# Four graph layers on one core: running sums of layers 1, 2 and 4 as scans over rows that ScalarE has turned

## The chip, the cores and the metric

One Trainium2 chip, one of its cores. The metric is the time of one execution of the program on the device, in microseconds (us); lower is better.

## The reference, cut to what matters

6250 nodes with 64 numbers each go through four layers; 106250 edges, sorted by destination, are shared by all. Each layer sums messages over the edges into a node, and the result is added to x and normalised.

```
x = _layernorm(x + _L0_gnn_ref(x, L0_gnn_weight, src, dst, edge_type_16), axis=-1)
x = _layernorm(x + _L1_gnn_ref(x, L1_gnn_beta, src, dst), axis=-1)
x = _layernorm(x + _L2_gnn_ref(x, edge_index, L2_gnn_W_l, L2_gnn_W_r, L2_gnn_att, L2_gnn_bias), axis=-1)
x = _layernorm(x + _L3_gnn_ref(x, L3_gnn_W, L3_gnn_coeff, L3_gnn_h_bias, L3_gnn_loop_weight, src, dst, edge_type_8), axis=-1)
...
    out = jax.ops.segment_sum(m, dst, num_segments=feat.shape[0])                         # L0: m = x[src] @ w[edge type]
    out = jax.ops.segment_sum(alpha[:, None] * x[col_index], row_index, num_segments=N)   # L1: softmax of cosines
    agg = jax.ops.segment_sum(msg, dst, num_segments=n_nodes)                             # L3: 2 bases x 64 numbers an edge
```

## The kernel before

The edges are padded to 128 x 832: each partition holds 832 edges in a row (columns), and the columns are worked on in 52 chunks of 16 (`CH`, `NCH`). A segment sum is a running sum along the columns that starts anew where `gf` is 0: row j becomes row j-1 times `gf[j]` plus the message of column j. The running sums are stored to DRAM (`s0` to `s3`), and the row at each node's last edge is fetched from there.

All order is fixed by hand: each engine has its own program, and semaphores (`S[...]`) join them. The names in this text count layers from 1; the code counts from 0 (`L0` to `L3`).

- **Layer 1**, `linear_chunk_g/_v/_y`. POOL issues 16 indirect DMAs a chunk (`gather`, L190), one a column, from the table `y0` into a ring of 8 chunk buffers (`ring0`, `N0`). DVE makes the running sum in place, 16 dependent instructions a chunk (L514), each of which waits for the one before by the semaphore `lin0`. SP stores the chunk. POOL may fill a buffer again once the chunk 8 before is stored and the first row of the chunk 7 before is summed. The first 5 chunks (`FR`) go another way, over TensorE. Beside chunks 5 to 30 DVE and TensorE count edges a node: `hist_v` (L364, L366), then 16 matmuls of `hist_t` (L372), two such steps a chunk, and DVE's next step waits for TensorE's last (semaphore `hpe0`). `twin_v` (L2062) are tests of symmetry, two a chunk to chunk 31.
- **Layer 2**, `layer1_v`. POOL gathers into 4 chunk buffers (`G1`). `fill1` (L779) spreads the destination's row over its edges (16 dependent instructions a chunk, in PSUM), `soft1` (9 steps, L800 to L820) makes the logits and the running maximum, ACT takes the exponential (`exp1_a`, L828), `px1` (L838, L839) multiplies, and `step1` (L850) is the running sum of 65 numbers, 16 dependent instructions. They are interleaved on DVE.
- **Layer 3** (`layer2_*`) is not touched.
- **Layer 4**, `basis_chunk_v`. POOL gathers into 4 chunk buffers (`GB`), which `L1663`, the product with the two coefficients of an edge type, sets free. Ahead of it stand L1650, L1652 and L1655 (the coefficients), behind it 16 dependent instructions of 128 numbers (L1673). Beside chunks 8 to 14 `loop3_v` takes in products of x that TensorE made (`turn3_t`, `turn3_a`, `loop3_t`).

The two steps of the code that matter most:

```
v.scalar_tensor_tensor(out=buf[:, j, :], in0=buf[:, j - 1, :] if j else prev[:, CH - 1, :],
                       scalar=gf[:, c * CH + j:c * CH + j + 1], in1=buf[:, j, :],
                       op0=ALU.mult, op1=ALU.add).then_inc(S["lin0"], 1)
```

## Time and profile before

| what | value |
|---|---|
| times without a profile, 3 runs | 6202.34 us median (6194.47 to 6212.94) |
| time of the profiled execution | 6149.63 us |
| its span, first to last instruction | 6147.8 us |
| DVE busy | 2871.9 us, 47% |
| POOL busy | 3520.1 us, 57% |
| PE busy | 1595.5 us, 26% |
| ACT busy | 1115.1 us, 18% |

The profiled execution is 52.7 us shorter than the median of the runs without a profile. No engine is busy throughout: a share of busy time is a mean over four layers with different limits, so each layer is to be read by itself, by what its engines wait for.

### The profile page before, as it was taken

How to read it: one execution, taken by the hardware profiler on the slowest of the kernel's cores; microseconds unless marked ns; L12 is line 12 of the kernel's file. 1: busy time of each engine (PE TensorE's matmuls, PEld its weight loads, DVE VectorE, ACT ScalarE, POOL GpSimd, SP SyncE). 2: the span in 40 equal slices, each digit the busy share in tenths (PEclk: the TensorE clock that was granted, in tenths of full speed). 3: DMA queues.
4: the chain of work that ended last, by engine and by line, in shares of the span. 5: the costliest groups of instructions: out<-in, count | busy, mean ns of one | idle time of the engine just before them, and what ended most of it. 6: DMA issues, size and time to landing. Idle time of an engine off the chain costs nothing.

```text
span 6147.8 us, 31588 instructions
## 1 busy us (share of the span) xinstructions
PE 1595.5 (26%) x6543; PEld 813.1 (13%) x6543; DVE 2871.9 (47%) x7562; ACT 1115.1 (18%) x3419; POOL 3520.1 (57%) x3636
## 2 busy tenths in 40 slices
PE   5531110000000000002375566666664500000002
PEld 1421110000000000001122222222221400000001
DVE  2344444125354455544255565555556632444344
ACT  1100000000000000001155555555555400000000
POOL 5355666766666666664634544454442576676754
PEclk7765555555555555556687888888887655555555
DMA  4212222221222222221123333333334221222222
GB/s 140 105 53 62 65 67 72 72 67 61 51 72 65 64 70 72 69 67 37 49 103 122 140 139 129 125 140 139 129 124 157 67 67 54 65 79 76 67 68 72
DMA packets 185944, 529.62 MB, mean 86 GB/s; under 512 B 70454, under 2 KB 75170, under 8 KB 169480
## 3 DMA queue, kind: packets, MB, share of 16 engines
q1 hardware_dynamic: 65816, 395.51, 17.0%
q0 software_dynamic: 117696, 129.81, 10.5%
q10 hardware_dynamic: 2224, 2.13, 0.1%
q14 instruction: 151, 1.24, 0.1%
q8 instruction: 57, 0.93, 0.1%
HBM read 185.57 MB, written 341.44 MB: 86 GB/s over the span
## 4 chain that ended last, share of the span: by engine, by line
DVE 39%; another core or an unknown queue 24%; issue 18%; PE 11%; ACT 5%; POOL 3%; DMA 1%; DVEq 0%; ACTq 0%; POOLq 0%; SPq 0%
DVE AR L1673 10%; DVE AR L514 5%; DVE ps L779 5%; PE ps L1220 4%; POOL AR L190 2%; PE ps L1236 2%; DVE AR L850 2%; DVE AR L1385 2%; ACT AR L1371 2%; DVE AR L364 1%; DVE AR L1663 1%; ACT AR L1227 1%; DVE AR L800 1%; PE ps L680 1%
## 5 line engine op out<-in xcount | busy, mean ns | idle before, releaser
L190 POOL DMA_INDIRECT AR<-xt,Si x2496 | 2402.0, 962 | 1687.3 <-issue 743.9
L190 POOL DMA_INDIRECT AR<-y,R x752 | 721.4, 959 | 520.9 <-issue 222.2
L1385 DVE SCALAR_TENSOR_TENSOR AR<-AR,gf 128x390 f32<-128x390 f32 x780 | 484.2, 621 | 654.3 <-ACT AR L1371 458.3
L1220 PE MATMUL ps<-AR,WLR 128*128 128x512 f32 x1248 | 681.7, 673 | 131.6 <-ACT AR L1227 88.2
L1673 DVE SCALAR_TENSOR_TENSOR AR<-AR,gf 128x128 f32<-128x128 f32 x831 | 295.0, 355 | 472.6 <-DVE AR L1673 360.1
L1371 ACT ACTIVATE AR<-AR 128x64 f32<-128x64 f32 x1664 | 495.5, 346 | 0.0
L1227 ACT ACTIVATE AR<-ps 128x512 f32<-128x512 f32 x624 | 368.5, 591 | 210.9 <-remote 146.7
L779 DVE SCALAR_TENSOR_TENSOR ps<-ps,gf,AR 128x64 f32<-128x64 f32 x831 | 242.2, 291 | 303.5 <-remote 160.5
L514 DVE SCALAR_TENSOR_TENSOR AR<-AR,gf 128x64 f32<-128x64 f32 x831 | 237.5, 286 | 258.2 <-DVE AR L514 155.5
L190 POOL DMA_INDIRECT AR<-s,endi x196 | 215.5, 1100 | 186.8 <-issue 112.4
L1220 PEld LDWEIGHTS ps<-AR,WLR 128*128 128x128 f32 x1248 | 238.8, 216 | 436.7 <-issue 312.5
L1354 DVE TENSOR_TENSOR AR<-AR,ps 128x512 f32<-128x512 f32 x416 | 282.8, 680 | 5.3 <-ACT ps L1329 5.3
L850 DVE SCALAR_TENSOR_TENSOR AR<-AR,gf 128x65 f32<-128x65 f32 x780 | 217.4, 279 | 100.7 <-remote 64.2
L1191 DVE SCALAR_TENSOR_TENSOR AR<-AR,gf 128x64 f32<-128x64 f32 x831 | 229.8, 277 | 48.4 <-DVE AR L1191 23.5
L364 DVE TENSOR_TENSOR AR<-AR,ps 128x1568 bf16<-128x1568 int32 x52 | 92.7, 1783 | 315.9 <-remote 291.4
L828 ACT ACTIVATE ps<-AR 128x17 f32<-128x17 f32 (+1 forms) x52 | 9.8, 188 | 1250.9 <-remote 431.8
L372 PE MATMUL ps<-AR 128*98 128x64 bf16 x832 | 80.1, 270 | 560.8 <-DVE AR L366 433.8
L1743 PE MATMUL ps<-ident,AR 128*128 128x128 f32 x1 | 0.5, 477 | 809.4 <-DVE AR L1673 809.4
L1992 ACT ACTIVATE AR<-AR 128x7 f32<-128x7 f32 x7 | 1.5, 208 | 1114.0 <-DVE AR L633 1067.9
L1236 PE MATMUL ps<-AR,A 128*32 128x512 f32 x1248 | 203.5, 604 | 0.0
L1016 PE MATMUL ps<-AR,ones 128*128 128x384 f32 (+1 forms) x6 | 3.7, 758 | 708.3 <-DVE AR L967 708.3
L1251 PE MATMUL ps<-ident,AR 128*128 128x128 f32 x208 | 55.3, 417 | 492.2 <-issue 319.1
(324 smaller groups left out, 2987.6 us busy)
## 6 DMA issues: line engine op xcount, KB each, us to landing
s<-AR SPq DMA_DIRECT2D x51, 3168.0 KB
AR<-xd SPq DMA_DIRECT2D x104, 512.0 KB
s<-AR SPq DMA_DIRECT2D x51, 1024.0 KB
AR<-xt,Si POOLq DMA_INDIRECT x2496
s<-AR SPq DMA_DIRECT2D x53, 512.0 KB
s<-AR SPq DMA_DIRECT2D x51, 528.0 KB
...
```

Of the source, the lines that this page charges most:

```text
L190: g.indirect_dma_start(out=o, out_offset=None, in_=table, in_offset=bass.IndirectOffsetOnAxis(ap=idx, axis=0)).then_inc(S[sem], 16)
L514: v.scalar_tensor_tensor(out=buf[:, j, :], in0=buf[:, j - 1, :] if j else prev[:, CH - 1, :], scalar=gf[:, c * CH + j:c * CH + j + 1], in1 ...
L779: v.scalar_tensor_tensor(out=xf1(c, j), in0=xf1(c, j - 1) if j else xf1(c - 1, CH - 1), scalar=gf[:, c * CH + j:c * CH + j + 1], in1=XBv[: ...
L850: v.scalar_tensor_tensor(out=Sv[:, j, 0:65], in0=Sv[:, j - 1, 0:65] if j else Sp[:, CH - 1, 0:65], scalar=gf[:, c * CH + j:c * CH + j + 1] ...
L1191: v.scalar_tensor_tensor(out=cur[:, j, D:P], in0=cur[:, j - 1, D:P] if j else prv[:, CH - 1, D:P], scalar=gf[:, c * CH + j:c * CH + j + 1] ...
L1220: t.matmul(PS[2 + k % 3][:], WLR[:, ch * P:(ch + 1) * P], XT2[:, u % 6, :], start=True, stop=True).then_inc(S["pm"], 1)
L1227: s.activation(RL2[:, u % 5, ch * 512:(ch + 1) * 512], PS[2 + k % 3][:], ACT.Relu).then_inc(S["ar"], 1)
L1236: m = t.matmul(PS[6][32 * q:32 * q + 32, :], w_, m_, start=(ch == 0), stop=(ch == 3))
L1354: v.tensor_tensor(s2v(c)[:, cols, 0:n * 65].rearrange("p j (h d) -> p j h d", h=n)[:, :, :, 0:D], bc(xsv(c)[:, cols, 0:D].unsqueeze(2), [P ...
L1371: s.activation(Sv[:, j, h * 65:h * 65 + D], xsv(c)[:, j, 0:D], ACT.Copy, scale=pe_[:, h, j:j + 1]).then_inc(S["ap"], 1)
L1385: m = v.scalar_tensor_tensor(out=Sv[:, j, 0:HW], in0=Sv[:, j - 1, 0:HW], scalar=gf[:, c * CH + j:c * CH + j + 1], in1=Sv[:, j, 0:HW], op0= ...
L1673: v.scalar_tensor_tensor(out=cur[:, j, :], in0=cur[:, j - 1, :] if j else prv[:, CH - 1, :], scalar=gf[:, c * CH + j:c * CH + j + 1], in1= ...
```

## The change

In layers 1 (from chunk 5 on), 2 and 4 a chunk's 16 dependent row instructions become few scans. A scan (`tensor_tensor_scan`) runs along 512 elements in memory, state times gate plus element. For that the 16 columns of one of the 64 features must lie side by side, so:

- `gates_a` (ACT) spreads a chunk's `gf` over a PSUM bank, 480 elements; element 0 of each group of 16 stays 0, set once by `memset`.
- `turned0_a`, `turned1_a` (ACT) copy a chunk of 1024 from (column, feature) to (feature, column). In layer 4, and for the sum of layer 2, no such copy is there: DVE's own product writes turned (L950, L1837 of the changed kernel; they answer to L838 and L1663).
- DVE adds the carry of the chunk before into column 0 (`carry0_v`, the first steps of `fill1` and `step1`, in `basis_v`), and then scans: 2 of 512 a chunk in layer 1; 2 for `fill1` and 2 and one of 16 for `step1` in layer 2; 4 in layer 4.
- `summed0_a`, `summed1_a`, `summed3_a` (ACT) copy the sums back to (column, feature), and SP stores when that copy is done (semaphore `co`) rather than when DVE's last row is.
- POOL fills a buffer of layer 1 again when the chunk 8 before is stored; it waits for nothing of the chunk 7 before. In layers 1 and 4 the last chunk is two units of 8 columns; in layer 2 its second half isn't taken apart from the first any more.
- ACT's program, which in layer 1 had nothing in this stretch and in layer 2 the exponentials alone, gets these copies; in layer 4 `turn3_a` moves in among them. DVE gets `memset`s of 11 PSUM banks. In layer 1 DVE's `hist_v` now stands behind the scans.

```diff
+        def gates_a(bank, at, n):
+            return s.copy(bank[:].rearrange("p (d j) -> p d j", j=n)[:, :, 1:n],
+                          bc(gf[:, at + 1:at + n].unsqueeze(1), [P, 512 // n, n - 1]))
+        def gates0_a(e, i):
...
+            if n == CH and i >= 2:
+                e.wait_ge(S["sc"], scans_upto(UN0, D, i - 1))
+            gates_a(gx0(i), c * CH + j0, n).then_inc(S["gx"], 1)
+        def turned0_a(e, i):
...
+            if i >= 2:
+                e.wait_ge(S["st"], i)
+            s.copy(t0v(i), ring0(c)[:, j0:j0 + n, :].rearrange("p j d -> p d j")).then_inc(S["cx"], 1)
+        def summed0_a(e, i):
+            c, j0, n = UN0[i]
+            e.wait_ge(S["sc"], scans_upto(UN0, D, i + 1))
+            s.copy(ring0(c)[:, j0:j0 + n, :], t0v(i).rearrange("p d j -> p j d")).then_inc(S["co"], 1)
+        def carry0_v(e, i):
+            c, j0, n = UN0[i]
+            e.wait_ge(S["cx"], i + 1)
+            if i:
+                e.wait_ge(S["sc"], scans_upto(UN0, D, i))
+                row = t0v(i - 1)[:, :, UN0[i - 1][2] - 1]
...
+            v.scalar_tensor_tensor(out=t0v(i)[:, :, 0], in0=row, scalar=gf[:, c * CH + j0:c * CH + j0 + 1],
+                                   in1=t0v(i)[:, :, 0], op0=ALU.mult, op1=ALU.add).then_inc(S["st"], 1)
+        def scan0_v(e, i):
...
+            for k in range(n * D // 512):
+                part = TT0[:, i % 2, k * 512:(k + 1) * 512]
+                v.tensor_tensor_scan(part, gx0(i)[:], part, 0.0, ALU.mult, ALU.add).then_inc(S["sc"], 1)
...
         def linear_chunk_g(e, tab, idx, c):
...
             if c >= N0:
                 e.wait_ge(S[f"s_{b}"], 16 * (c // N0))
-                e.wait_ge(S["lin0"], lin_at(c - N0 + 1, 0))
+                if c - N0 + 1 < FR:
+                    e.wait_ge(S["lin0"], lin_at(c - N0 + 1, 0))
+                elif c - N0 + 1 == FR:
+                    e.wait_ge(S["st"], 1)
...
+        def summed1_a(e, c):
+            e.wait_ge(S["sc"], raised("sc", 1) + 3 * (c + 1))
...
+                s.copy(Sv[:, j:j + n, 0:65], sum1(c)[:, :, j:j + n].rearrange("p d j -> p j d")).then_inc(S["co"], 1)
...
+            v.tensor_tensor_scan(PS[2 * (c % 2) + i - 1][:], gx1(c)[:], TX1[:, c % 2, (i - 1) * 512:i * 512], 0.0,
+                                 ALU.mult, ALU.add).then_inc(S["f1"], 1)
...
-            v.tensor_tensor(Sv[:, :, 0:D], Gv[:, :, 0:D], bc(pe_.unsqueeze(2), [P, CH, D]), ALU.mult).then_inc(S["p1"], 1)
...
+            v.tensor_tensor(sum1(c)[:, 0:D, :].rearrange("p d j -> p j d"), Gv[:, :, 0:D],
+                            bc(pe_.unsqueeze(2), [P, CH, D]), ALU.mult).then_inc(S["p1"], 1)
...
+            lo, n = (i - 1) * 512, 512 if i < 3 else CH
+            part = SUM1[:, c % 2, lo:lo + n]
+            v.tensor_tensor_scan(part, gx1(c)[:, 0:n], part, 0.0, ALU.mult, ALU.add).then_inc(S["sc"], 1)
...
             if c >= NBUF:
-                e.wait_ge(S["m3"], 4 * (c - NBUF + 1))
+                e.wait_ge(S["m3"], c - NBUF + 1)
...
+        def basis_v(e, i):
...
+            v.tensor_tensor(sum3(i).rearrange("p (b d) j -> p j b d", b=NBS), bc(rows.unsqueeze(2), [P, n, NBS, D]),
+                            bc(CW3[:, i % 2, :, 0:n].rearrange("p b j -> p j b").unsqueeze(3), [P, n, NBS, D]),
+                            ALU.mult).then_inc(S["m3"], 1)
...
+            for k in range(n * W3 // 512):
+                part = SUM3[:, i % 2, k * 512:(k + 1) * 512]
+                v.tensor_tensor_scan(part, gx3(i)[:], part, 0.0, ALU.mult, ALU.add).then_inc(S["sc"], 1)
+                if more and k == 0:
+                    weight3_v(e, i + 1, 2)
...
             for c in range(NCH):
-                exp1_a(e, c)
+                if c + 2 < NCH:
+                    gates1_a(e, c + 2)
+                    turned1_a(e, c + 2)
+                if c + 1 < NCH:
+                    exp1_a(e, c + 1)
+                summed1_a(e, c)
...
-            for q in range(NG):
-                turn3_a(e, q)
+            gates3_a(e, 0)
+            for i, (c, j0, n) in enumerate(UN3):
+                if 6 <= c < 6 + NG:
+                    turn3_a(e, c - 6)
+                if i + 1 < len(UN3):
+                    gates3_a(e, i + 1)
+                summed3_a(e, i)
...
+            for bank in (2, 3, 4, 5):
+                v.memset(PS[bank][:], 0.0).then_inc(S["init"], 1)
```

DVE's program in layer 1 beside the counting of edges, before; `k_hpe0` is TensorE's signal, `k_g_5` the landing of a gather:

```order
L364 TENSOR_TENSOR AR<-AR,ps 128x1568 [waits k_hpe0]
L366 TENSOR_TENSOR AR<-AR,ps 128x1024
L364 TENSOR_TENSOR AR<-AR,ps 128x1568 [waits k_hpe0]
L366 TENSOR_TENSOR AR<-AR,ps 128x1024
L2062 SCALAR_TENSOR_TENSOR AR<-AR 128x832 [waits k_v] x2
L514 SCALAR_TENSOR_TENSOR AR<-AR,gf 128x64 [waits k_lin0,k_g_5]
L514 SCALAR_TENSOR_TENSOR AR<-AR,gf 128x64 [waits k_lin0] x15
```

The same place in the changed kernel, from one carry to the next (the scans are printed as SCALAR_TENSOR_TENSOR of 512; L2257 and L2254 are tests of the kind of L2062):

```order
L546 SCALAR_TENSOR_TENSOR AR<-AR,gf 128x64 [waits k_sc,k_cx]
L2257 TENSOR_SCALAR AR<-Dd 128x832
L2254 TENSOR_SCALAR AR<-AR 128x832 [waits k_v]
L555 SCALAR_TENSOR_TENSOR AR<-ps,AR 128x512 [waits k_gx,k_st]
L555 SCALAR_TENSOR_TENSOR AR<-ps,AR 128x512
L365 TENSOR_TENSOR AR<-AR,ps 128x1568 [waits k_hpe0]
L367 TENSOR_TENSOR AR<-AR,ps 128x1024
L365 TENSOR_TENSOR AR<-AR,ps 128x1568 [waits k_hpe0]
L367 TENSOR_TENSOR AR<-AR,ps 128x1024
```

The 16 rows of L514 are gone; in their place stand a carry, which waits for ACT's turned copy (`k_cx`), and two scans; the counting moved behind them.

ACT's program in layer 1 in the changed kernel, three chunks of 47; before, no row stands there:

```order
L515 COPY ps<-gf 128x32x15 [waits k_sc,k_init]
L530 COPY AR<-AR 128x1024 [waits k_st,k_g_1]
L535 COPY AR<-AR 128x1024 [waits k_sc]
L515 COPY ps<-gf 128x64x7 [waits k_init]
L530 COPY AR<-AR 128x1024 [waits k_st,k_g_2]
L535 COPY AR<-AR 128x1024 [waits k_sc]
```

Each L535 waits for DVE's scans of its chunk (`k_sc`), and the next chunk's L530 is behind it.

DVE's program in layer 4, one chunk before:

```order
L1650 TENSOR_TENSOR ps<-AR,ps 128x128 [waits k_m3]
L1652 TENSOR_TENSOR AR<-ps,co 128x256 [waits k_m3]
L1655 TENSOR_REDUCE ps<-AR 128x32 [waits k_m3]
L1663 TENSOR_TENSOR AR<-AR,ps 128x2048 [waits k_m3,k_s_1,k_g_3]
L1673 SCALAR_TENSOR_TENSOR AR<-AR,gf 128x128 [waits k_lin3,k_m3]
L1673 SCALAR_TENSOR_TENSOR AR<-AR,gf 128x128 [waits k_lin3] x15
```

and one chunk of the changed kernel:

```order
L1837 TENSOR_TENSOR AR<-AR,ps 128x16x128 [waits k_co,k_cf,k_g_2]
L1806 TENSOR_TENSOR ps<-AR,ps 128x128
L1845 SCALAR_TENSOR_TENSOR AR<-AR,gf 128x128 [waits k_sc,k_m3]
L1809 TENSOR_TENSOR AR<-ps,co 128x256 [waits k_cf]
L1855 SCALAR_TENSOR_TENSOR AR<-ps,AR 128x512 [waits k_gx,k_st]
L1812 TENSOR_REDUCE ps<-AR 128x32 [waits k_cf]
L1855 SCALAR_TENSOR_TENSOR AR<-ps,AR 128x512 x3
```

The product (L1837) no longer has the coefficients' three steps ahead of it: those of the next chunk (L1806, L1809, L1812) stand between its carry and its scans.

## Rows read from the trace of the kernel before

**Rows 1.** By stretch: us; busy PE, PEld, DVE, ACT, POOL (instructions); clock, DMA, GB/s.
```profile
416.00:1041.00 625.00, 77.76 (x809) 71.00 (x808) 296.67 (x581) 0.00 (x0) 378.15 (x400) 0.50 0.22 63
1041.00:1403.00 362.00, 1.20 (x4) 1.00 (x4) 104.85 (x372) 0.00 (x0) 236.43 (x240) 0.50 0.27 84
1543.00:2802.00 1259.00, 1.46 (x4) 1.00 (x4) 626.70 (x2244) 16.88 (x104) 787.70 (x833) 0.50 0.26 66
2802.00:4867.00 2065.00, 1223.03 (x4694) 546.88 (x4694) 1129.32 (x2752) 1018.71 (x3133) 990.93 (x983) 0.79 0.34 117
4867.00:6062.00 1195.00, 30.32 (x123) 26.03 (x123) 477.07 (x1059) 3.85 (x13) 796.96 (x832) 0.50 0.23 68
```

**Rows 2.** Timeline of POOL around the counting of edges: start, us, what [idle before].
```profile
1028.70 0.94 POOL L190 DMA_INDIRECT AR<-y,R  x1 [0.30 <-issue]
1029.95 0.94 POOL L190 DMA_INDIRECT AR<-y,R  x1 [0.30 <-issue]
1041.59 0.94 POOL L190 DMA_INDIRECT AR<-y,R  x1 [10.69 <-DVE AR L514]
```

**Rows 3.** What POOL waited for in layers 1, 2 and 4: us, times, longest.
```profile
POOL AR L190 <- DVE AR L514: 140.8, 18, 15.1
...
POOL AR L190 <- DVE AR L839: 181.1, 16, 18.3
...
POOL AR L190 <- DVE AR L1663: 115.4, 15, 21.2
```

**Rows 4.** Timeline of POOL: first fetch of nodes' rows behind layers 1, 2, 4.
```profile
1406.58 1.03 POOL L190 DMA_INDIRECT AR<-s,endi  x1 [55.73 <-issue]
...
2804.25 0.94 POOL L190 DMA_INDIRECT AR<-s,fixg  x1 [40.25 <-DMA s<-AR]
...
6064.70 0.94 POOL L190 DMA_INDIRECT AR<-s,endi  x1 [34.55 <-DMA s<-AR]
```

**Rows 5.** By short stretch: us; busy DVE (instructions); clock, DMA, GB/s.
```profile
1111.00:1313.00 202.00, 41.19 (x145) 0.50 0.24 67
1383.00:1403.00 20.00, 17.54 (x62) 0.50 0.56 223
1708.00:1749.00 41.00, 11.23 (x39) 0.50 0.18 36
1749.00:1762.00 13.00, 12.72 (x47) 0.50 0.37 112
4972.00:5084.00 112.00, 36.22 (x80) 0.50 0.23 64
5386.00:5414.00 28.00, 25.88 (x58) 0.50 0.30 98
```

**Rows 6.** Timeline of DVE, counting of edges and sums.
```profile
1011.42 1.21 DVE L366 TENSOR_TENSOR AR<-AR,ps 128x1024 bf16<-128x1024 int32 x1
1035.71 1.79 DVE L364 TENSOR_TENSOR AR<-AR,ps 128x1568 bf16<-128x1568 int32 x1 [23.08 <-remote]
...
1040.56 5.13 DVE L514 SCALAR_TENSOR_TENSOR AR<-AR,gf 128x64 f32<-128x64 f32 x16
```

**Rows 7.** Groups of DVE by line: count, busy us, mean ns, idle before.
```profile
L1314 DVE TENSOR_TENSOR_SCAN AR<-AR 128x96 f32<-128x96 f32 x52 | 18.2, 350 | 0.0
...
L810 DVE TENSOR_TENSOR_SCAN AR<-Bn,AR 128x16 f32<-128x16 f32 x52 | 9.8, 189 | 18.1 <-remote 13.8 <-issue 2.2 <-DVE AR L807 2.0
...
L838 DVE TENSOR_TENSOR AR<-AR,ps 128x1024 f32<-128x1024 f32 x52 | 63.0, 1211 | 0.3 <-ACT AR L829 0.2 <-issue 0.2
```

**Rows 8.** Groups of ACT by line: contiguous and strided copies.
```profile
L1212 ACT COPY AR<-ps 128x512 f32<-128x512 f32 x208 | 122.0, 587 | 78.6 <-remote 28.3 <-PE ps L1205 27.9 <-issue 20.3
...
L1335 ACT COPY AR<-AR 128x96 f32<-128x96 f32 x52 | 18.1, 348 | 0.0
L1330 ACT ACTIVATE AR<-AR 128x102 f32<-128x102 f32 x51 | 14.0, 274 | 0.0
```

**Rows 9.** Timeline of the PE's counting step.
```profile
1012.69 1.54 PE L372 MATMUL ps<-AR 128*98 128x64 bf16 x16 [8.37 <-DVE AR L366]
```

More of the change, by code:

```diff
@@ L614, in stored_all @@
         def stored_all(e, L, n):
-            more = (16, 48, 48, 16)[L]
+            more = (16, 16, 48, 16)[L]
             for b in range(n):
@@ L1624, in build @@
         E8 = arena(6200, NC).bitcast(I32)
+        UN3 = [(c, 0, CH) for c in range(NCH - 1)] + [(NCH - 1, 0, CH // 2), (NCH - 1, CH // 2, CH // 2)]
+        W3 = NBS * D
+        SUM3 = arena(9100, 2, CH * W3)
         OH3 = PS[0][:, 64:64 + CH * R3].rearrange("p (j r) -> p j r", r=R3)
@@ L1677, in basis_chunk_y @@
-        def basis_chunk_y(e, c):
-            n = CH // 2 if c == NCH - 1 else CH
-            for j in range(0, CH, n):
-                e.wait_ge(S["lin3"], lin_at(c, j + n - 1))
-                load(e, columns_view(s3, c * CH + j, n), s3v(c)[:, j:j + n, :].rearrange("p j d -> p (j d)"), f"s_{c % 3}")
+            at = c * CH + j0
+            rows = GB[:, b, :].rearrange("p (j d) -> p j d", j=CH)[:, j0:j0 + n, :]
+            more = i + 1 < len(UN3)
+            if j0:
+                e.wait_ge(S["late"], 16 * CH + 16 * n)
+            else:
+                e.wait_ge(S[f"g_{b}"], gathered_before(3, b) + 16 * CH * (c // NBUF) + 16 * n)
@@ new lines, in basis_v @@
+            if i:
+                e.wait_ge(S["sc"], raised("sc", 3) + scans_upto(UN3, W3, i))
+                v.scalar_tensor_tensor(out=sum3(i)[:, :, 0], in0=sum3(i - 1)[:, :, UN3[i - 1][2] - 1],
+                                       scalar=gf[:, at:at + 1], in1=sum3(i)[:, :, 0],
+                                       op0=ALU.mult, op1=ALU.add).then_inc(S["st"], 1)
+            if more:
+                weight3_v(e, i + 1, 1)
+            if i:
+                e.wait_ge(S["st"], raised("st", 3) + i)
@@ L1868, in _ @@
                 load(e, rows_view(xt3, sl), X[:, sl, :].rearrange("p l d -> p (l d)"), "xt")
-            for c in range(NCH):
-                basis_chunk_y(e, c)
+            for i in range(len(UN3)):
+                basis_chunk_y(e, i)
             for q, (l0, n) in enumerate(G3):
@@ L1989, in _ @@
                 raw_first_a(e, u)
+            gates0_a(e, 0)
+            for i in range(len(UN0)):
+                if i + 1 < len(UN0):
+                    gates0_a(e, i + 1)
+                turned0_a(e, i)
+                summed0_a(e, i)
             for q in range(NG):
@@ L2116, in _ @@
                 linear_chunk_v(e, c)
+            for bank in (2, 3, 4, 5):
+                v.memset(PS[bank][:], 0.0).then_inc(S["init"], 1)
             masks_v(e, vc, 0)
```

346 lines of the change are left out of this document (221 added, 125 removed), and 2 rows, old and new, of the table names.

## The prediction

> **What bounds the kernel now.** I read the busy time by stretch first. In layers 1, 2 and 4 no engine is near full: POOL is the busiest with 0.61, 0.63 and 0.67 of its stretches, DVE has 0.47, 0.50 and 0.40 [rows 1]. Layer 3 (2802 to 4867 us) is the only one where TensorE and ACT work hard, and the change does not touch it. So the question for the other three is whether POOL's busy share is its limit. The timeline of POOL says it is: gathers start every 1.25 us (0.94 busy, 0.30 of issue) with nothing waited for [rows 2]. A layer of 832 gathers therefore takes at least 832 x 1.25 = 1040 us, a chunk of 16 takes 20.0 us. The chunks take 21.0 us in layer 1 ((1403 - 416) / 47), 24.2 in layer 2 (1259 / 52) and 23.0 in layer 4 (1195 / 52) [rows 1]. The excess is POOL waiting for a buffer that DVE has not set free, 140.8, 181.1 and 115.4 us [rows 3], and a tail after the last gather: POOL's first fetch of nodes' rows comes 55.7, 40.3 and 34.6 us later [rows 4]. These six numbers, 568 us, are all that faster sums can win.
>
> Why does DVE fall behind at half its time busy? DVE alone, in short stretches, shows two paces [rows 5]. With POOL stopped or just started again: 62 instructions in 20 us, 47 in 13, 58 in 28, so 0.32, 0.28 and 0.48 us each, their own durations. With POOL at its full pace for some 20 us and more: 145 in 202 us, 39 in 41, 80 in 112, so 1.39, 1.05 and 1.40 us each, though the instructions last no longer. In that slow pace an instruction costs about 1.0 to 1.4 us whatever it does, unless it lasts longer itself. I don't know why, and need only that the price is by the instruction. TensorE feels it too: its 16 matmuls of a counting step are recorded in 1.54 us [rows 9], yet DVE's next step started 23.08 us later, 4.8 us after POOL's last gather (1030.9 to 1035.7), and POOL then stood for 10.69 us until DVE had a row summed [rows 2, 6]. That pattern comes back about every 50 us and two chunks to 1040 us, and sets layer 1's first part.
>
> **The change part by part.** The number of DVE instructions falls, and they get longer.
>
> A scan of 512 is not in the trace. Scans of 16 and 96 last 189 and 350 ns [rows 7], 2.0 ns an element; 350 + 416 x 2.0 = 1.18 us is the value I take. Bounds: 0.8 us (at 1.18 ns an element, L838's 1211 ns for 1024 [rows 7]) and 2.4 us (twice).
>
> ACT's copies: 512 contiguous elements out of PSUM last 587 ns [rows 8], so 0.55 us for the 480 gates and at least 1.1 us for 1024. A strided copy of 96 elements lasts 348 ns, a contiguous activation of 102 lasts 274 [rows 8]: if some 0.19 us of both is fixed, 1.65 against 0.82 ns an element. The turned copies read or write at strides of 16 and 64 numbers, so I take 1.9 us for 1024, 3.6 for 2048, bounds 1.1 and 1.9 below. The same doubt holds for DVE's products that now write turned (L838, 1211 ns for 1024 [rows 7], and L1663 with 2048, so about 2.3): no loss to twice, 1.2 and 2.3 us more a chunk; I take half. A rule bears on this: the Trainium skill, SBUF — State Buffer, in "Door 1: The DMA port swizzle", says that SBUF is read in lines of 16 bytes and that each access which moves to another line costs, with a stride of four fp32 as the limit. It speaks against the change: by it every turned copy and product pays in full. ACT's two rows agree with it as far as they go; no row here shows DVE at such a stride.
>
> *Layer 1, chunks 5 to 30, with the counting.* Removed a chunk: 16 row instructions, 5.1 us in the fast pace [rows 6]. Added: carry 0.3, two scans 2.4. But the counting steps stay, and DVE waits for TensorE in them as before, until POOL pauses. POOL may now go one chunk further before it pauses (it needs the store of the chunk 8 before, not a row of the chunk 7 before), and after the pause it waits for carry, scans, ACT's copy back and the store, some 12 us instead of 6. So a cycle is 4.8 + 12 + 20 for each chunk, 57 us for two or 77 for three, 25.6 to 28.5 a chunk against 25 now; the chunk gained in the ring is worth 20 us once. I set this part at nothing; bounds: 60 us lost (three more a chunk, less the 20) and 100 won (if DVE is through before the slow pace sets in).
>
> *Layer 1, chunks 31 to 51.* Now 16 x 1.39 = 22.2 us a chunk, a little over POOL's 20.0. After: 3 instructions of DVE (4.2 us) and 3 of ACT (about 2 each), one behind the other, 10 to 12 us. POOL goes on at its pace, which it mostly has here already, and the backlog that makes the tail is gone: carry, scan, copy back, store for half a chunk, about 8 us instead of 55.7. Won: 47 us.
>
> *Layer 2.* DVE's instructions a chunk fall from 43 to 19 (4 and 4 in place of 16 and 16; 11 stay). Slow pace: 19 x 1.05 = 20 to 19 x 1.4 = 27 us, against 43 x 1.05 = 45 now. Fast: about 11.5 us of durations. So DVE is at or a little over POOL's 20.0 in the slow pace; it loses some 2 to 7 us a chunk, the ring of four takes that up for 10 chunks or more, then a short pause brings the fast pace, in which DVE makes up a chunk. I leave 45 of 181.1 us of waiting: won 136. ACT's five copies and exponentials (some 5 us, each dispatched apart) have a chunk's time; the turned copy of chunk c+2 is asked for after four of DVE's steps of chunk c, about when it is ready. Tail: nine short steps, exponential, product, scans, copy, store, about 15 us instead of 40.3: won 25. Together 161; bounds 80 and 195.
>
> *Layer 4.* Slow pace now: 20 instructions x 1.40 = 28 us a chunk. After: product 2.3 to 4.6, eight others x 1.4 = 11.2, so 14 to 16 us, under 20.0. POOL is the bound except for chunks 8 to 14. There TensorE's products (22 instructions for each), ACT's `turn3_a`, which now stands ahead of the gates for the next chunk, and `loop3_v` follow one another, about 25 to 30 us a chunk in the slow pace; the ring takes up 60 of it. I leave 35 of 115.4: won 80. Tail: half a product, carry, two scans, copy, store, about 10 instead of 34.6: won 25. Together 105; bounds 40 and 135.
>
> *Added.* 11 `memset`s of a PSUM bank, some 0.6 us each like a DVE operation of 512: 6 us if nothing hides them. Layer 3 and the node stages move but keep their length.
>
> Sum: 47 + 161 + 105 - 6 = 307 us. Against the profiled execution's own time, 6149.6 us, that is 5843 us. The median without a profile is 52.7 us above it, and I carry that over: 5895 us.
>
> **The rivals.**
>
> *The waits go further than I say.* If DVE slips through the counting cycles and the ring takes up layer 4's middle, up to 100 + 35 + 45 us more are won: 5720 to 5790. For it: the cycle has slack of few us. Against: TensorE's step is untouched and takes the wait over.
>
> *Strided work and ACT eat the gain.* Twice the time for scans, products and copies adds in layer 2 about 8 us a chunk to DVE; DVE is then at 28 to 35 us in the slow pace and waits come back: layer 2 wins 60, layer 4 50, layer 1 20: about 6070. This is what the rule above would make of it if DVE pays in full and more. Against: even so DVE has fewer steps than now.
>
> *Slower.* Now the chain of layer 1's sums never leaves DVE. After, each chunk goes ACT, DVE, ACT. If ACT's signal is held as TensorE's is in the counting, until POOL pauses and 4.8 us more [rows 2, 6], then every chunk costs 20.0 + 4.8 + some 2 us. The mean over the three layers is (987 + 1259 + 1195) / 151 = 22.8 us a chunk, which is where it decides; at 26.8 the kernel takes 151 x 4.0 = 600 us more, 6800 us. For it: TensorE's 23.08 us is real. Against: DVE's own signals came after 1.4 us in the same pace, TensorE has 32 instructions behind its one signal and ACT one; in layer 3 POOL gathers too and ACT does 3133 instructions in 2065 us [rows 1], though POOL is at 0.48 there.
>
> *It does nothing.* If the slow pace is by work and not by instruction, half the instructions at double length cost the same. Against: in layer 4's slow stretch an instruction is busy for 36.22 / 80 = 0.45 us and in its fast one for 25.88 / 58 = 0.45 us [rows 5]; the work is the same, only the time between steps is not.
>
> **How the numbers follow.** Main case 0.72, time 5790 to 6010. Further gain 0.08; strided work and ACT 0.12; slower 0.06; nothing 0.02. The range 5760 to 6060 takes in the first two and half of the third, and leaves 0.16 out. 0.3% (19 us) is about what a measurement of this kernel can tell from no change. Faster by more: 0.72 + 0.08 + 0.12, less a little for mishaps of its parts: 0.91. Within: 0.02. Slower: 0.07.
>
> **What would show it.** Right: POOL's starts 1.25 us apart through most of layers 2 and 4, the waits for L839 and L1663 down to some 45 and 35 us; first fetch of nodes' rows 8 to 15 us after the last gather; in the counting part still gaps of about 20 us ahead of `hist_v`; scans of 512 near 1.18 us. Wrong: if scans or turned products last over 2.4 us, if ACT's copies wait for each other so that DVE idles ahead of the carry, or if DVE after the change stands for ACT 20 us at a time. Above all my price by the instruction comes from stretches where DVE's steps depend on each other; if independent steps pay less, layer 2 wins more.

## The result, and the profile after

| | before | after |
|---|---|---|
| median, us | 6198.41 (6193.02 to 6212.94, 4 runs) | 6108.82 (6079.91 to 6118.44, 4 runs) |
| ratio | | 0.9841, 95% interval 0.9809 to 0.9874 |
| profiled execution / its span, us | 6149.63 / 6147.8 | 6079.91 / 6077.9 |

Faster, as forecast, but by 90 us where 303 were forecast: 6108.8 lies above the range (5760 to 6060). In the profiled pair the gain is 69.9 us of span; the profiled execution after lies 28.9 us below its median, so neither figure is exact to more than some 20 us.

By stretch, as [rows 1], shifted to where the same work now lies (us; busy PE, PEld, DVE, ACT, POOL; clock, DMA share, GB/s):

```profile
416.00:1070.00 654.00, 78.51 (x816) 71.79 (x816) 249.06 (x258) 105.98 (x75) 389.43 (x408) 0.50 0.21 61
1070.00:1366.00 296.00, 1.20 (x4) 1.00 (x4) 60.30 (x84) 86.86 (x63) 218.94 (x225) 0.50 0.31 97
1526.00:2717.00 1191.00, 2.25 (x6) 1.50 (x6) 562.35 (x1003) 241.84 (x262) 792.95 (x832) 0.50 0.27 70
2717.00:4817.00 2100.00, 1233.83 (x4692) 548.76 (x4692) 1127.00 (x2745) 1021.32 (x3131) 990.92 (x983) 0.78 0.33 115
4817.00:5980.00 1163.00, 31.33 (x125) 26.58 (x125) 493.28 (x501) 218.00 (x121) 836.36 (x833) 0.50 0.24 71
```

What POOL waited for in layer 1, and in layer 2, and in layer 4 from 4960 to 5960 us (us, times, longest), to set beside [rows 3]:

```profile
POOL AR L191 <- DMA s<-AR: 143.0, 8, 21.4
...
POOL AR L191 <- remote: 123.1, 20, 7.0
...
POOL AR L191 <- issue: 236.8, 711, 0.9
POOL AR L191 <- DVE AR L1837: 41.5, 3, 23.7
```

POOL's first fetches of nodes' rows, to set beside [rows 4]:

```profile
1371.02 1.55 POOL L191 DMA_INDIRECT AR<-s,endi  x1 [9.81 <-issue]
...
2719.10 0.94 POOL L191 DMA_INDIRECT AR<-s,fixg  x1 [27.98 <-DMA s<-AR]
...
5979.78 0.95 POOL L191 DMA_INDIRECT AR<-s,endi  x1 [11.26 <-DMA s<-AR]
```

The groups that the price list was about, to set beside [rows 7, 8]:

```profile
L1855 DVE TENSOR_TENSOR_SCAN AR<-ps,AR 128x512 f32<-128x512 f32 x208 | 242.5, 1208 | 156.6 <-issue 91.2 <-ACT ps L515 65.3
L950 DVE TENSOR_TENSOR AR<-AR,ps 128x1024 f32<-128x1024 f32 x52 | 98.7, 1898 | 0.1
L1837 DVE TENSOR_TENSOR AR<-AR,ps 128x2048 f32<-128x2048 f32 (+1 forms) x53 | 187.0, 3529 | 509.4 <-DMA AR<-xt,Si 509.4
...
L1796 ACT COPY AR<-AR 128x2048 f32<-128x2048 f32 (+1 forms) x53 | 189.3, 3572 | 725.6 <-issue 448.8 <-DVE AR L1855 276.8
L530 ACT COPY AR<-AR 128x1024 f32<-128x1024 f32 (+1 forms) x48 | 90.6, 1888 | 134.1 <-DMA AR<-y,R 134.1
L515 ACT COPY ps<-gf 128x480 f32<-128x480 f32 x153 | 85.4, 559 | 29.9 <-DVE ps L1024 17.9 <-DVE ps L2320 8.8 <-DVE ps L2421 3.2
```

The prices are close to those taken (scan 1.21 us, copies 1.89 and 3.57, gates 0.56, products 1.90 and 3.53 where I had about 1.8 and 3.4). So the loss lies elsewhere, and a ledger finds it. Each line of the table is the time between two fetches of POOL, before from [rows 2, 4] and the first gathers of layers 2 and 4 (1543.8 and 4867.4 us), after from the timeline above and the first gathers (1526.2 and 4817.8).

| stretch | before | after | gain | forecast |
|---|---|---|---|---|
| layer 1, to the nodes' fetch | 1406.6 | 1371.0 | 35.6 | 41 (47 less 6) |
| nodes behind layer 1 | 137.2 | 155.2 | -18.0 | 0 |
| layer 2 with its tail | 1260.5 | 1192.9 | 67.6 | 161 |
| nodes, layer 3, nodes | 2063.2 | 2098.7 | -35.5 | 0 |
| layer 4 with its tail | 1197.3 | 1162.0 | 35.3 | 105 |
| the rest, to the end of the span | 83.1 | 98.1 | -15.0 | 0 |

Layer 4 is the odd line. DVE hardly holds POOL up there: it waits for gathers 509.4 us (L1837, above), POOL waits for DVE 41.5 us, all before 5233 us. POOL's waits fell from 115.4 to 41.5 us, close to the 35 that I had left, and yet POOL needs 1162 us for work that I had put at 1040. The same queries in two halves of a stretch in which POOL waits for nothing, in the kernel after:

```profile
5233.00:5475.00 242.00, 0.00 (x0) 0.00 (x0) 135.68 (x136) 61.52 (x30) 183.66 (x192) 0.50 0.30 94
5475.00:5945.00 470.00, 0.00 (x0) 0.00 (x0) 194.03 (x189) 85.75 (x42) 349.57 (x336) 0.50 0.24 70
```

192 gathers in 242 us are 1.26 us each; 336 in 470 us are 1.40. The 1.40 is a mean: in a held chunk of 16, which takes 22.4 us, some gathers still start 1.25 us apart and others 1.40 to 2.1, so two rows of a timeline don't show it. The same split stands in the kernel before, behind the last pause of layer 1, and I had not looked:

```profile
1041.00:1262.00 221.00, 1.20 (x4) 1.00 (x4) 58.27 (x208) 0.00 (x0) 166.77 (x177) 0.50 0.27 79
1262.00:1350.00 88.00, 0.00 (x0) 0.00 (x0) 17.85 (x63) 0.00 (x0) 68.81 (x64) 0.50 0.24 71
```

177 gathers at 1.25, then 64 at 1.375 (the window begins a little before the slower pitch does; the last chunks take 22.4 us here too). This gives the theory that I tested.

**Theory A, a long-run limit.** A gather costs 1.40 us in the long run. At 1.25 us POOL runs ahead of that by 0.15 us a gather; after 11 or 12 chunks (some 190 gathers, 28 us ahead) it is held at 1.40, until a pause lets it run ahead again. While it is ahead, each DVE instruction costs 1.40 us (the theory as I tested it; the changed kernel's layer 4 goes against this part, see below). **Rivals:** B, 1.25 us is the floor and DVE's slow steps are what lengthens the layers, by the signal (B0), by the instruction (B1) or by their work (B2); C, DVE bounds layer 2 and only a longer pause makes it fast; D, the turned copies and products take the gain.

### The profile page after: what moved, and what is told of

The parts are those of the page before. It is cut to its first block and busy times, and to the rows that moved or that the text cites. A ratio compares the mean times of both kernels' runs of the same rounds, so it can differ in the third digit from the quotient of the medians.

```text
span 6077.9 us, 30032 instructions
## 1 busy us (share of the span) xinstructions
PE 1605.7 (26%) x6543; PEld 814.5 (13%) x6543; DVE 2732.0 (45%) x5146; ACT 1755.8 (29%) x3826; POOL 3568.6 (59%) x3636
## 3 DMA queue, kind: packets, MB, share of 16 engines
q0 software_dynamic: 117696, 129.81, 10.6%
## 5 line engine op out<-in xcount | busy, mean ns | idle before, releaser
L191 POOL DMA_INDIRECT AR<-xt,Si x2496 | 2447.7, 981 | 1605.6 <-issue 778.7
L1355 PE MATMUL ps<-AR,WLR 128*128 128x512 f32 x1248 | 696.1, 686 | 135.8 <-ACT AR L1362 95.7
L1837 DVE TENSOR_TENSOR AR<-AR,ps 128x2048 f32<-128x2048 f32 (+1 forms) x53 | 187.0, 3529 | 509.4 <-DMA AR<-xt,Si 509.4
L1796 ACT COPY AR<-AR 128x2048 f32<-128x2048 f32 (+1 forms) x53 | 189.3, 3572 | 725.6 <-issue 448.8
L1855 DVE TENSOR_TENSOR_SCAN AR<-ps,AR 128x512 f32<-128x512 f32 x208 | 242.5, 1208 | 156.6 <-issue 91.2
L535 ACT COPY AR<-AR 128x1024 f32<-128x1024 f32 (+1 forms) x48 | 90.0, 1875 | 644.6 <-DVE AR L555 494.8
L1326 DVE SCALAR_TENSOR_TENSOR AR<-AR,gf 128x64 f32<-128x64 f32 x831 | 230.1, 277 | 48.8 <-DVE AR L1326 24.6
```

The lines of the kernel that those rows point to most:

```text
L191: g.indirect_dma_start(out=o, out_offset=None, in_=table, in_offset=bass.IndirectOffsetOnAxis(ap=idx, axis=0)).then_inc(S[sem], 16)
L1326: v.scalar_tensor_tensor(out=cur[:, j, D:P], in0=cur[:, j - 1, D:P] if j else prv[:, CH - 1, D:P], scalar=gf[:, c * CH + j:c * CH + j + 1] ...
L1355: t.matmul(PS[2 + k % 3][:], WLR[:, ch * P:(ch + 1) * P], XT2[:, u % 6, :], start=True, stop=True).then_inc(S["pm"], 1)
L1796: s.copy(s3v(c)[:, j0:j0 + n, :], sum3(i).rearrange("p x j -> p j x")).then_inc(S["co"], 1)
L1837: v.tensor_tensor(sum3(i).rearrange("p (b d) j -> p j b d", b=NBS), bc(rows.unsqueeze(2), [P, n, NBS, D]), bc(CW3[:, i % 2, :, 0:n].rearra ...
L1855: v.tensor_tensor_scan(part, gx3(i)[:], part, 0.0, ALU.mult, ALU.add).then_inc(S["sc"], 1)
```

## The experiments

The first pair of traces and the six groups of runs below were each taken on a chip of their own, and the occasions are of two kinds: the kernel before took 6198, 6056, 6049 and 6144 us on four of these occasions and 4809 on three. I call the first kind of chip limited and the second quiet, but no chip was met twice, so these runs can't tell a property of the chip from a condition of the occasion; on one of the quiet chips a single one of 31 executions of the kernel before took 6614 us. Each run below is compared with the kernel before on its own chip.

The kept traces of the two kinds also differ in what they hold. A trace lists the updates of semaphores: there are 18726 to 23540 such records in each trace from a limited chip, and 75610 to 77676 in each from a quiet one, for the same numbers of DMAs and much the same instructions. In the held stretch above (5475 to 5945 us) there are 671, one every 0.70 us, for 336 gathers; in 500 us of the same kernel on a quiet chip there are 6999, for 398 gathers. So on limited chips updates either merge or go unrecorded, and it may be the recording itself that takes 0.70 us an event. That rival stands untested: none of these runs compares an execution that was recorded with one that wasn't.

Lengths of layers in the text run from POOL's first gather to the first fetch of nodes' rows behind it, by POOL's timeline of each run.

**1. Signals and instructions of DVE in layer 2** (limited chip, before 6056.14 us). `sig2` and `sig124` leave out signals whose waiters can take the next one:

```diff
-            v.tensor_tensor_scan(part, gx1(c)[:, 0:n], part, 0.0, ALU.mult, ALU.add).then_inc(S["sc"], 1)
+            m = v.tensor_tensor_scan(part, gx1(c)[:, 0:n], part, 0.0, ALU.mult, ALU.add)
+            if i == 3:
+                m.then_inc(S["sc"], 1)
...
-            m.then_inc(S["q1"], 1)
+            if i:
+                m.then_inc(S["q1"], 1)
```

> Same instructions as the changed kernel, but in layer 2 DVE signals 13 times a chunk instead of 18 (first half of the first product, the second product, the first scan of each group and the second of the last group signal no longer; who waited for them waits for the next signal of DVE). Theory A, the price is by the signal: in layer 2 the slow chunk of DVE took 26.63 us = 19 x 1.40; it falls by 5 x 1.40 to about 19.6 us, under POOL's 20.0 us a chunk, POOL's waits in layer 2 (123.1 and 28.0 us) fall under 40 and the kernel takes about 6000 us. Theory B, the price is by the instruction, or by the work: the slow chunk stays at 26.6 us and the time at 6109 +- 15 us.

> As sig2, and the scans of layers 1 and 4 signal once a chunk instead of two and four times. Theory A: as sig2 in layer 2; in layer 4 DVE already waits for POOL, so only a change of POOL's 22.4 us a chunk there could show, and if that pace comes from DVE's signals (9 a chunk, then 6) it falls toward 20.0 in the last 23 chunks, up to 50 us less than sig2. If it has another cause, sig124 equals sig2 within 20 us. Theory B: 6109 +- 15 us.

Measured: 5979.74 us (ratio 0.9871, 0.9836 to 0.9906) and 5986.76 (0.9878, 0.9843 to 0.9912). The slow chunk of DVE stays at 26.6 us in both (in parts of the layer every second one is 18.9), layer 2 takes 1198 and 1197 us, layer 4 1160 and 1160. The price is not by the signal, and layer 4's pace not DVE's doing. The unchanged kernel after was not run on this chip; the comparison is of chunks and layers with its first trace, and of the runs with each other.

`dumsig` and `dumno` add four one-element copies a chunk, with and without a signal:

```diff
+                for k in range(4):
+                    m = v.tensor_copy(dm[:, 4 * c + k:4 * c + k + 1], gf[:, 4 * c + k:4 * c + k + 1])
+                    m.then_inc(S["du"], 1)
```

> The changed kernel with four more DVE copies of one element a partition in each chunk of layer 2, each with a signal that nobody waits for. Theory A (by the signal): the slow chunk grows by 4 x 1.40 = 5.6 to 32.2 us, the kernel by some 200 to 280 us. Theory B1 (by the instruction): the same here, and the same in dumno. Theory B2 (by the work): the chunk grows by 4 x 0.06 us or so, the kernel by 0 to 15 us.

> The same four copies a chunk without signals. Theory A: the slow chunk stays near 26.6 us, the kernel grows by 0 to 15 us. Theory B1 (by the instruction): slow chunk 32.2 us, 200 to 280 us more. Theory B2: as A.

Measured: 5979.27 and 5968.84 us, one run each. In both the slow chunk grows from 26.6 to 32.2 us, by 4 x 1.40. Two slow stretches, `dumno` and then the kernel after:

```profile
1640.00:1672.20 32.20, 0.00 (x0) 0.00 (x0) 11.27 (x24) 4.62 (x5) 24.27 (x27) 0.50 0.25 59
```
```profile
1846.10:1872.70 26.60, 0.00 (x0) 0.00 (x0) 10.95 (x19) 4.63 (x5) 15.13 (x16) 0.50 0.23 56
1972.00:1982.10 10.10, 0.00 (x0) 0.00 (x0) 10.06 (x21) 4.61 (x6) 7.66 (x9) 0.50 0.43 129
```

19 instructions at 1.40 us are 26.6, 23 are 32.2 (the window also catches one of the next chunk); the last row is a chunk in the fast pace (with two of its neighbours' instructions). So in layer 2 B1's price is right, signal or none, but the 200 to 280 us that B1 put on the kernel did not come: both runs are within 11 us of `sig2`. The Trainium skill, VectorE: DVE Perf Modes, "The DRAIN you can't avoid", says that a semaphore behind each instruction adds nothing to a chain of DVE copies; these two runs agree, 32.2 us with and without. No theory of DVE's pace had the next number: layer 2 takes 1194 and 1193 us, as with chunks of 26.6. DVE's slow chunk got 5.6 us longer and the layer no longer. Something else fixes its length.

**2. A chip of the other kind** (before 4809.46 us). The unchanged kernel after, one one-byte memset behind each gather of layers 1, 2 and 4 in both kernels, and the copies and products contiguous (which then sums other elements):

```diff
                 gather(buf[:, j, :], xt3, Si[:, c * CH + j:c * CH + j + 1],
                        "late" if c == NCH - 1 and j >= CH // 2 else f"g_{b}")
+                g.memset(fl[:, 1 * flat[0]:1 * flat[0] + 1], 0)
+                flat[0] += 1
```
```diff
-            s.copy(tx1(c), XB1[:, c % 3, :].rearrange("p (j d) -> p d j", j=CH)).then_inc(S["cx"], 1)
+            s.copy(TX1[:, c % 2, :], XB1[:, c % 3, :]).then_inc(S["cx"], 1)
```

> The changed kernel once more, beside the others on their chip. Layers 1, 2 and 4 as in its first trace (1179, 1193 and 1162 us from first gather to the nodes' fetch); layer 3 was 2099 us there and 1997 to 2012 us in the four later runs whose layer 3 is the same code, so the time is expected at 5975 +- 25 us if layer 3 goes by the chip, 6100 if it goes by the kernel.

> The changed kernel with one POOL memset of one byte a partition behind each gather of layers 1, 2 and 4, so that gathers start some 1.35 to 1.5 us apart instead of 1.25. Theory A (backlog): in the long run a gather costs 1.40 us; at 1.25 POOL runs ahead by 28 us in 11 to 12 chunks, and while it is ahead every DVE instruction costs 1.40 us and TensorE's signals wait. Then with gathers 1.40 apart DVE never turns slow (chunk of 10 us in layer 2), the counting costs 22 to 24 us a chunk instead of 26.2, layers 2 and 4 keep their length within 30 us if the pitch is 1.40 to 1.43, and the time falls by 50 to 120 us; if the pitch is 1.5, each layer takes 832 x 1.5 = 1250 us and the time rises by up to 80. Theory B (1.25 is what a gather costs, DVE is slow while gathers run): DVE stays slow at 26.6 us a chunk and each layer gains 832 x 0.15 or more: 250 to 400 us slower.

> The same memset behind each gather in the kernel before. Theory A: DVE's 43 instructions a chunk in layer 2 take 12 us in the fast pace, its 16 row instructions of layer 4 10 us, so the kernel before becomes as fast as pace1 within 40 us. Theory B: DVE's slow chunks of 45 and 28 us stay, the kernel is at least 250 us slower than before.

> The changed kernel with ACT's copies and DVE's products of layers 1, 2 and 4 written and read contiguously instead of turned; the sums are then taken over other elements. Rival that strided work eats the gain: copies fall from 1.9 and 3.6 us to about 1.1 and 2.1, products from 1.9 and 3.5 to 1.2 and 2.3, and the time falls by 60 to 150 us. Theory A: POOL's 22.4 us a chunk stay, the time stays within 20 us.

Measured: after 4815.52 us (ratio 1.0010, 1.0001 to 1.0020), `pace1` 4817.14 (1.0014), `bpace1` 4811.08 (1.0002), `cont` 4814.95 (1.0011). My guess that layer 3 alone differs by chip was wrong: everything does. Two stretches of the kernel after on this chip, layer 2 and layer 4:

```profile
1205.00:2242.00 1037.00, 1.46 (x4) 1.00 (x4) 516.66 (x977) 235.06 (x257) 783.84 (x831) 0.50 0.31 79
3700.00:4745.00 1045.00, 31.32 (x125) 26.57 (x125) 493.27 (x498) 216.45 (x119) 783.09 (x823) 0.50 0.27 78
```

831 gathers in 1037 us: 1.25 us each to the end, the 1040 us of my floor. POOL waits for no buffer in layers 1, 2 and 4, DVE is never slow, the recorded signals of DVE in layer 2 come 0.01 us after the instruction's end (median), and the kernels before and after are equal to 0.1%. The memset fits into the 0.30 us between gathers, so `pace1` and `bpace1` told nothing of theory A. `cont` settles rival D for this kind of chip: turned against contiguous, copies take 1888 against 1025 ns and 3565 against 1865, products 1864 against 1214 and 3520 against 2247, and the time is the same. The Trainium skill, SBUF — State Buffer, "Door 1: The DMA port swizzle", is borne out in the durations (a factor of 1.5 to 1.9 beyond its stride) and costs nothing here: ACT and DVE have room under POOL's pace. `cont` was not run on a limited chip.

**3. Pacing POOL on a limited chip** (before 6049.37 us). Three memsets behind each gather, in both kernels; and a wait for two chunks' buffers at once:

```diff
+                for u in range(3):
+                    m = g.memset(fl[:, 3 * (c * CH + j) + u:3 * (c * CH + j) + u + 1], 0)
```
```diff
-                e.wait_ge(S["p1"], 2 * (c - 3))
+                e.wait_ge(S["p1"], 2 * (c - 3 + (c % 2 == 0)))
```

> The changed kernel again, as the measure for the other three on their chip. On a chip like that of the second call (4809 us for the kernel before, POOL's gathers 1.25 us apart throughout, signals 0.01 us late) it equals the kernel before within 0.3%. On a chip like that of the first two traces (signals at multiples of 0.70 us) it takes 1.2 to 1.6% less than the kernel before.

> The changed kernel with three one-byte POOL memsets behind each gather of layers 1, 2 and 4 (with one, they fitted into the 0.30 us between gathers and the pitch stayed at 1.25 us). Gathers then start about 1.40 to 1.6 us apart. On a chip of the slow kind: theory A (a gather costs 1.40 us there in the long run, POOL runs ahead at 1.25, and while it is ahead DVE pays 1.40 us an instruction and TensorE's signals wait): DVE is fast throughout layer 2 (10 to 12 us a chunk), the counting takes POOL's pace instead of 26.2 us a chunk, and with a pitch of p the three layers take about 832 x p each; at 1.45 the kernel is 20 to 80 us faster than without the memsets. Theory B (DVE is slow whenever gathers run): DVE's slow chunks of 26.6 us stay and the kernel is 250 us or more slower. On a chip of the quiet kind both expect 832 x (p - 1.25) more for each layer and nothing else.

> The same three memsets in the kernel before. Slow kind of chip, theory A: DVE fast throughout, so the kernel equals pace3 within 40 us and is faster than the kernel before by 60 to 150 us. Theory B: slower than the kernel before by 250 us or more. Quiet kind: as pace3.

> The changed kernel with POOL's wait in layer 2 taken for two chunks at once: ahead of every even chunk it waits until DVE has set free the buffers of two. Pauses become rarer and longer (12 us and more instead of 6.6). Slow kind of chip, theory A: the sum of the pauses is set by the 1.40 us a gather, so layer 2 keeps its 1193 us within 25, though DVE turns fast at other places. Theory C (a longer pause is what makes DVE fast, and DVE is what bounds the layer): layer 2 gets 40 to 100 us shorter. Quiet kind: nothing changes, within 20 us.

| | us | ratio to before | layer 1's counting ends | nodes 1 | layer 2 | layer 4 | rest |
|---|---|---|---|---|---|---|---|
| after_third | 5983.95 | 0.9895 (0.9860 to 0.9930) | 1073 | 154 | 1196 | 1159 | 97 |
| pace3 | 5917.94 | 0.9783 (0.9746 to 0.9821) | 938 | 138 | 1194 | 1183 | 83 |
| bpace3 | 5918.45 | 0.9789 (0.9757 to 0.9822) | 942 | 137 | 1193 | 1184 | 82 |
| pair | 5971.77 | 0.9873 (0.9840 to 0.9907) | 1084 | 154 | 1191 | 1160 | 98 |

The kernel after, unchanged, gains 1.05% here, a little less than the 1.2 to 1.6% that I had expected.

Adding 7,248 instructions to POOL makes both kernels faster, and makes them equal. Layers 2 and 4 in `pace3`, then in `bpace3` (a gather and three memsets are four POOL instructions):

```profile
1475.00:2607.00 1132.00, 0.00 (x0) 0.00 (x0) 498.27 (x942) 226.82 (x249) 901.06 (x3200) 0.50 0.27 69
4665.00:5815.00 1150.00, 30.16 (x122) 25.89 (x122) 484.57 (x487) 214.30 (x117) 922.56 (x3257) 0.50 0.24 70
```
```profile
1485.00:2620.00 1135.00, 1.46 (x4) 1.00 (x4) 583.76 (x2142) 16.23 (x100) 914.25 (x3197) 0.50 0.27 69
4664.00:5817.00 1153.00, 25.68 (x104) 22.09 (x104) 471.39 (x1049) 3.17 (x10) 924.34 (x3257) 0.50 0.24 70
```

3200 / 4 = 800 gathers in 1132 us, 1.415 each, with scans and (799 in 1135, 1.42) with row steps. POOL waits for no buffer in either; DVE, which has twice the instructions in `bpace3`, keeps up in both. The memsets themselves would make the pitch 1.27 us; here is `pace3` in layer 4, at that pitch and then held:

```profile
5600.28 0.94 POOL L192 DMA_INDIRECT AR<-xt,Si  x1
5601.23 0.17 POOL L1837 MEMSET fl<- 128x1 uint8 x3
5601.55 0.94 POOL L192 DMA_INDIRECT AR<-xt,Si  x1
5602.49 0.18 POOL L1837 MEMSET fl<- 128x1 uint8 x3
5603.32 0.95 POOL L192 DMA_INDIRECT AR<-xt,Si  x1 [0.65 <-issue]
5604.27 0.12 POOL L1837 MEMSET fl<- 128x1 uint8 x1
5605.21 0.10 POOL L1837 MEMSET fl<- 128x1 uint8 x1 [0.83 <-issue]
```

So with memsets POOL is held at 1.40 on the mean from the second chunk of a layer on, and never runs ahead; why they make it so I can't say. The rest follows theory A. DVE steps keep up, TensorE's signals come through (the counting's steps mostly follow one another every 11 to 13 us, where in the kernel after four come 5 to 7 us apart and then two of 27) and layer 1's first part ends 135 us earlier. Layer 2 keeps its length, layer 4 loses 24 us, about the 28 us ahead that it now starts without. `pair` agrees too: with pauses up to 13.5 us instead of 7.0, layer 2 takes 1191 us. That is against rival C, and so is `pace3`, where DVE is fast throughout and layer 2 is no shorter.

**4. What the 1.40 us belongs to, and the price of the remedy.** Layer 4's gathers fetch 64 rows from the fifth chunk on (the other 64 partitions keep old rows); the three memsets in layer 1 alone; `pace3` again:

```diff
-                gather(buf[:, j, :], xt3, Si[:, c * CH + j:c * CH + j + 1],
+                h = P if c < NBUF else P // 2
+                gather(buf[0:h, j, :], xt3, Si[0:h, c * CH + j:c * CH + j + 1],
```

> The changed kernel whose gathers of layer 4 fetch 64 rows instead of 128 from the fifth chunk on (the other 64 partitions keep older rows, so layer 4's result is another). On a chip of the slow kind: if the 1.40 us belongs to the rows of a gather (10.9 ns each), a half gather costs 0.70 us in the long run, POOL is never held and the chunks stay at 20 us or less throughout, so layer 4 takes some 50 us less than the 1160 us of the others. If it belongs to the gather, or to the POOL instruction, chunks turn to 22.4 us after 11 or 12 chunks as before and layer 4 keeps 1160 +- 15 us. On a quiet chip only the gather's own length shows.

> The changed kernel with the three memsets behind each gather of layer 1 alone. Theory A on a slow chip: layer 1 as in pace3 (1126 us instead of 1181), the nodes behind it as in pace3 (138 instead of 154), layers 2 and 4 as without memsets (1194 and 1160): 5905 to 5925 us, 0.990 of the changed kernel. If the gain of pace3 came from layers 2 or 4, it stays at 5984. On a quiet chip: 0 to 40 us slower than the kernel before.

> pace3 once more. Slow chip: 0.978 of the kernel before again. Quiet chip (1.25 us a gather without end): its pitch of 1.27 us costs 832 x 0.02 x 3 = 50 us at most, so 4810 to 4870 us.

Quiet chip, before 4809.28 us: 4777.20 (layer 4 1018 us, 19.3 a chunk to the end), 4826.51 (1.0035, 1.0022 to 1.0047) and 4856.34 (1.0096, 1.0079 to 1.0113). The remedy costs 1% where there is no limit. The first two once more:

> As half4, on another chip if one is met. On a chip of the slow kind: if the 1.40 us belongs to the rows of a gather (10.9 ns each), chunks of layer 4 stay at 20 us or less from the fifth on and layer 4 takes some 50 us less than 1160; if it belongs to the gather, chunks of 22.4 us come back and layer 4 keeps 1160 +- 15 us. On a quiet chip it repeats 4777 us.

> As pace_l1. Slow chip, theory A: 0.978 or less of the kernel before (layer 1 at 1126 us, the nodes behind it at 138, layers 2 and 4 at 1194 and 1160). If the gain of pace3 came from layers 2 or 4, about 0.989. Quiet chip: 1.0035 again.

Quiet again, before 4809.03: 4773.18 and 4830.84 (1.0046, 1.0029 to 1.0063). And the first a third time:

> As half4, hoping for a chip that shows the long-run limit. There, if the 1.40 us belongs to the rows of a gather (10.9 ns each), chunks of layer 4 stay at 20 us or less from the fifth on and layer 4 takes some 50 us less than 1160; if it belongs to the gather, chunks of 22.4 us come back and layer 4 keeps 1160 +- 15 us. On a quiet chip it repeats 4775 us and leaves the question open.

A limited chip, before 6143.94, this 6041.49 us. Layer 4 behind its last pause:

```profile
5195.00:5350.00 155.00, 0.00 (x0) 0.00 (x0) 98.19 (x99) 45.23 (x22) 115.70 (x129) 0.50 0.27 91
5370.00:5885.00 515.00, 0.00 (x0) 0.00 (x0) 212.46 (x207) 93.93 (x46) 385.93 (x369) 0.50 0.18 59
```

Half gathers come 1.20 us apart for 129 gathers, then 1.396 us apart (369 in 515), with half the rows, and layer 4 takes 1161 us as with full ones. The limit belongs to the gather, not to its rows. The DMA packets of a gather did not become fewer, though: POOL's queue has 117696 of them in this run as in the kernel after, with 117.22 MB in place of 129.81. A limit by the packet isn't told apart from one by the gather. Half gathers reach it sooner: 0.2 us ahead a gather times 129 is 26 us, where the full ones had 0.15 times 190, 28 us. `pace_l1` has met no limited chip, so what it would do on one is open.

## Why the prediction was wrong in size

Of the 237 us by which the profiled pair missed the forecast of 307, 163 are in layers 2 and 4, 68.5 in the stages that I had put at nothing, and 5 in layer 1.

**The floor (first paragraph): this step failed.** I took "gathers start every 1.25 us" from two rows [rows 2] and made it 1040 us a layer and 568 us that faster sums can win. On this kind of chip 832 gathers take 832 x 1.40 less the 28 us that POOL may be ahead, 1137 us. Against that, layer 4's 1163 us before, first gather to last, had 26 us to win, and layer 2's 1220 had 83, not the waits of 115 and 181 [rows 3]: the rest of each wait could only come back as longer gathers. In layer 4 it did, over 336 of them; layer 2 after takes 1165 us and layer 4 1151.

**DVE's two paces.** Where DVE was slow, the price by the instruction held: 19 x 1.40 = 26.6 us and 23 x 1.40 = 32.2 us in layer 2, 20 x 1.40 = 28 us in layer 4 before (the 43 of layer 2 before stayed near 1.05 each [rows 5]). It is no price for every instruction, though. I had 14 to 16 us a chunk for layer 4 and 4.2 us for layer 1's three instructions. In the changed kernel DVE's nine instructions of a layer 4 chunk follow one another without a gap and take 9.2 us, with POOL at 1.25 us a gather (129 in 162 us) and later at 1.40; layer 1's three take 2.7:

```profile
5294.00:5456.00 162.00, 0.00 (x0) 0.00 (x0) 74.10 (x73) 32.67 (x16) 122.75 (x129) 0.50 0.26 78
5395.10:5404.30 9.20, 0.00 (x0) 0.00 (x0) 9.12 (x9) 0.00 (x0) 6.97 (x8) 0.50 0.13 26
```

So the slow pace came where DVE had 16 or more instructions for each 20 us of gathers, and not where it had 9 or 3; no run looks for the border. That "a short pause brings the fast pace" did not hold: layer 2 has twelve slow chunks at first, and then seven to nine between one fast stretch and the next, the last of them with pauses of 6.6 us. But by `dumno`, `pair` and `bpace3` this costs little, so it isn't what failed.

**Layer 1.** Counting: I set it at nothing, with a cycle of 57 us for two chunks or 77 for three. It is 79 for three, with waits for stores of up to 21.4 us, 143.0 us in all where it had been 140.8; 654 us for 408 gathers against 625 for 400 are 25.6 and 25.0 us a chunk, within the bounds. The tail went from 55.7 to 9.8 us, 46 of the 47 taken. The nodes behind it gave back 18 us and the rest behind layer 4 gave back 15, where both tails were cut and where I had said that the node stages keep their length: this term, put at nothing without a reason, failed too. With the paced kernels both stand at 138 and 83 again with tails as short. That POOL now enters them with its lead unspent is argued from this, not shown by a run of its own.

**Layer 2.** 161 forecast, 67.6 measured: waits 181.1 to 123.1 (I had 45), the time from the first gather to the last 55 us shorter (I had 136), the tail 40.3 to 28.0 (I had 15).

**Layer 4.** 105 forecast, 35.3 measured: 23.3 in the tail (25 taken) and 12 of the 80 in front of it, though the waits themselves fell by 74. For chunks 8 to 14 I had 25 to 30 us a chunk; three of them took some 50. The matmuls end at 5045.54 us, and ACT's copy, with the gates behind it, and DVE's scans start 39 to 40 us later, though POOL makes no pause:

```profile
5044.43 1.11 PE L1870 MATMUL ps<-ident,X 128*128 128x128 f32 x4
...
5084.74 0.63 ACT L1878 COPY AR<-ps 128x384 f32<-128x384 f32 x2 [45.78 <-issue]
...
5085.93 1.22 DVE L1855 TENSOR_TENSOR_SCAN AR<-ps,AR 128x512 f32<-128x512 f32 x1 [39.96 <-issue]
```

That is one of my signs of being wrong, DVE standing for ACT 20 us at a time. It cost little: POOL waited 41.5 us and got about 28 us of them back as gathers at 1.25 us.

**Layer 3.** 35.5 us longer with the same code, some 31 of them in the layer itself and 4 in the nodes ahead of it, at a granted clock of 0.78 against 0.79 [rows 1]. On the other limited chips kernels with the change took 1996 to 2053 us there. The one other pair of traces from one limited chip is `pace3` with 1996 us and `bpace3` with 1986, so with memsets about 10 us go with the change. Without them no second pair tells, and the cause of the 35.5 us stays open.

**The rivals.** "Strided work and ACT eat the gain" gave the time nearest to the result (6070) by a mechanism that the runs don't show: contiguous work changed nothing on a quiet chip, and on limited ones layer 4 is bound by POOL. That it is near is luck. "Slower", ACT's signal held until POOL pauses, did not come; TensorE's signals were held, in layer 4 as well. None of my cases was that POOL has a second, slower pace of its own. And by its own chances the range left out 0.14, not 0.16.

**The sign.** Faster was right, on the kind of chip where it was measured. On limited chips the change gives 0.9841 and 0.9895 (and 0.9871 with the small edit of `sig2`); on a quiet one it gives 1.0010. As far as these runs tell, its gain is that DVE, with fewer instructions, is slowed less while POOL is ahead, and where POOL never gets ahead there is nothing to gain. `pace3` is the fastest version on the one limited chip where it ran (0.978) and 1% slower on a quiet one; `bpace3` does as well without the change.
